# Window attention: row scores in one piece over four PSUM banks, and TensorE's loop run to the last group

## The chip, the cores and the metric

The kernel runs on one core of one Trainium2 chip. The metric is the time of one execution on the device, in microseconds (us); three executions give a median of 966.29 us (965.54 to 969.62). Engines are named as the profile names them: PE is the matrix engine (TensorE), PEld its weight loads, DVE is VectorE, ACT is ScalarE, POOL is GpSimd, SP is SyncE.

## The reference

The input x is 4 images of 128 channels, 112 x 112 pixels, float32. Each image is normalised in 32 groups of 4 channels. Then it is shifted by 3 pixels down and across, cut into 7 x 7 windows (49 tokens, 256 windows an image), and each window goes through attention with 8 heads of 16 channels; the result is shifted back and added to x.

```
def _L0_conv_ref(x, w_qkv, b_qkv):
    xs = jnp.roll(x, (-SHIFT, -SHIFT), axis=(-2, -1))
    qkv = jnp.einsum('bchw,oc->bohw', xs, w_qkv) + b_qkv[None, :, None, None]
    ...
    scores = jnp.einsum('bxyhqd,bxyhkd->bxyhqk', q, k) * scale
    attn = jax.nn.softmax(scores, axis=-1)
    out = jnp.einsum('bxyhqk,bxyhkd->bxyhqd', attn, v)
    ...
    return jnp.roll(out, (SHIFT, SHIFT), axis=(-2, -1))
...
x = x + _L0_conv_ref(_gn(x), L0_conv_w_qkv, L0_conv_b_qkv)
```

## The kernel before

The unit of work is a group: half of a band of windows, 8 windows of 49 tokens, 392 tokens in all. There are 128 groups (4 images, 16 bands, 2 halves), numbered g. The channels lie on the 128 partitions, as 4 pairs of heads of 32 partitions each. Precision is kept by splitting a float32 value into a high and a low float16 (or bfloat16) half, and three products stand for one.

Every engine has its own program: a function `step(g, ...)` that does its share for several groups at different stages, so that groups overlap like in a pipeline. The first and last steps are written out (with plain Python numbers, where `live` leaves out groups that do not exist), those between stand in a hardware loop (`Fori`) of two steps. Engines meet only through semaphores; each engine takes its instructions strictly in the order written, so a waiting instruction holds up all that stand behind it. The stages of a group:

- ACT `normalise` (L347) scales the pixels into xn, POOL `split_x` (L270) splits it in halves.
- PE `project_q`, `project_k`, `project_v` (L701, L695, L708) make q, k and v in PSUM. q and k share one bank (QK_BANK, 4) one after the other; ACT `evac_q`, `evac_k`, `evac_v` bring them out, DVE `low_q` (L557) takes q's low half, DVE `mask_q` (L562) lays q out twice, with the odd and with the even head of each pair put to zero, and POOL `split_k` (L279) splits k.
- PE `row_scores` (L722): scores with queries on the partitions, which serve for the maximum over the keys alone. A matmul takes the 32 rows of one pair of heads (a row tile of the array), 49 columns. One pair of heads fills one PSUM bank with its 8 windows. It is done in two pieces j = 0 and 1, two pairs of heads each, in the same banks 0 and 1. DVE `maximum` (L571) reduces each piece; piece 1 cannot start before the maximum of piece 0 is read.
- POOL `split_max` (L288), in two instructions (L293 and L296), PE `turn_max` (L738) and ACT `evac_neg` (L366) bring the negated maxima into a layout by columns.
- PE `column_scores` (L743): the scores again, transposed (keys on the partitions), on 32 x 64 tiles of the array, and on top of them (L760) the negated maxima. COL_BANKS are 6 and 7 for the first two pairs of heads and 2 and 3 for the others. ACT `exp` (L371) makes the probabilities, one call for each pair of banks.
- PE `sum_keys` (L765) sums over the keys, DVE `invert` (L577) takes the reciprocal, ACT `high_inverse` and DVE `low_inverse` split it, PE `spread_inverse` (L790) spreads it to all channels.
- PE `weigh` (L777) multiplies the probabilities with v into banks 6 and 7; ACT `evac_even` (L387), DVE `join` (L587) and DVE `scale_rows` (L595) put it together, POOL `add_image` (L299) adds x, and SP stores the band.

The order of PE's step (L801 to L822) is v(g), sums(g-2), turn(g-1), weigh(g-2), q(g+1), row scores 0 of g, inverse(g-2), column scores(g-1), row scores 1 of g, k(g+1). So three groups are in work on PE, and the maxima of g are used in the step after.

DVE also collects the statistics of the next image (`take_stats`, one chunk a step), and in four steps before an image ends it works out its normalisation in small dependent operations (`change_image`, L639), the first of them `gather_channels` (L511). SP loads the band of the image after next into a slot when the band there is stored.

## Time and profile before

| | |
|---|---|
| Median of three executions | 966.29 us |
| The profiled execution's own time | 967.17 us |
| Its span, first to last instruction | 965.3 us |
| PE busy | 897.0 us, 93% |
| PEld busy | 724.3 us, 75% |
| DVE busy | 738.2 us, 76% |
| ACT busy | 656.9 us, 68% |
| POOL busy | 597.7 us, 62% |
| DMA queue of SP | 51.59 MB, 15.1% of the 16 engines' span |
| Mean granted clock of PE | 0.986 of full speed |

Busy time is the union of an engine's instructions; matmuls are pipelined, so a busy PE tells only that there was always one under way. In the page's chain of waits, which goes back from the last instruction to what released each, 86% of the span is PE's. The first 36 us go to loading and to the statistics of the first image, in which PE has little to do.

### The profile page before, as it was taken

The page shows a single profiled execution, that of the slowest core. Times are in us where ns is not written, and L with a number is a line of the kernel's source. Part 1 is how long each engine was busy: PE and PEld are TensorE (multiplying, and loading weights), DVE is VectorE, ACT ScalarE, POOL GpSimd, SP SyncE. Part 2 cuts the span into 40 slices and gives each one's busy share as a digit, 9 for nine tenths or more (in the row PEclk, how much of TensorE's full clock was granted, in tenths as well). Part 3 has the DMA queues.
Part 4 walks back from the last instruction along what each step waited for, and adds up shares of the span by engine and source line. Part 5 has one row for each costly group of instructions (what it writes and reads, how often), then busy time and mean ns, then how long its engine had stood idle before and what let it go on. Part 6 is the DMA issues. An engine that isn't in the chain of part 4 may idle for free.

```text
span 965.3 us, 104413 instructions
## 1 busy us (share of the span) xinstructions
PE 897.0 (93%) x46595; PEld 724.3 (75%) x46595; DVE 738.2 (76%) x1404; ACT 656.9 (68%) x1297; POOL 597.7 (62%) x1067
## 2 busy tenths in 40 slices
PE   0479999999999999999999999999999999999984
PEld 0258888887788888888778888888778888888863
DVE  6667787877878787878878787878877777777762
ACT  1346777776677777777677777777677777777752
POOL 1335666666566767676576767676666767676741
PEclk9999999999999999999999999999999999999996
DMA  9401112112112211221121000000000000000011
GB/s 372 170 4 51 50 67 67 51 49 67 51 49 67 67 53 47 67 67 54 46 67 50 17 33 33 33 17 33 34 17 33 33 33 17 33 33 33 17 36 37
DMA packets 29920, 51.96 MB, mean 54 GB/s; under 512 B 3650, under 2 KB 28868, under 8 KB 29764
## 3 DMA queue, kind: packets, MB, share of 16 engines
q1 hardware_dynamic: 29892, 51.59, 15.1%
q8 instruction: 17, 0.28, 0.1%
q14 instruction: 11, 0.09, 0.0%
HBM read 25.89 MB, written 25.69 MB: 53 GB/s over the span
## 4 chain that ended last, share of the span: by engine, by line
PE 86%; DVE 8%; issue 4%; POOL 1%; ACT 1%; DMA 0%; POOLq 0%; SPq 0%; DVEq 0%; ACTq 0%
PE psum L733 16%; PE psum L785 12%; PE psum L753 11%; PE psum L771 10%; PE psum L717 8%; PE psum L705 8%; PE psum L698 7%; PE psum L797 4%; PE psum L760 3%; PE psum L713 3%; PE psum L740 2%; DVE neg_max L574 2%; DVE stats L494 2%; DVE q_halves L559 1%; DVE mixed L599 1%
## 5 line engine op out<-in xcount | busy, mean ns | idle before, releaser
L374 ACT ACTIVATE probs_t<-psum,exp_scale 128x800 f32<-128x800 f32 x256 | 223.6, 925 | 177.8 <-PE psum L760 177.8
L574 DVE TENSOR_REDUCE neg_max<-psum 100x16 f32<-100x784 f32 x256 | 249.5, 974 | 43.1 <-PE psum L733 18.3
L293 POOL TENSOR_SCALAR neg_halves<-neg_max 100x32 bf16<-100x32 f32 x128 | 60.5, 473 | 289.9 <-DVE neg_max L574 289.9
L733 PEld LDWEIGHTS psum<-k_hi,q_masks 32*128 32x128 f16 x8192 | 174.7, 91 | 47.6 <-issue 46.4
L733 PE MATMUL psum<-k_hi,q_masks 32*128 32x49 f16 x8192 | 197.4, 179 | 4.5 <-issue 2.7
L733 PE MATMUL psum<-k_lo,q_masks 32*128 32x49 f16 x4096 | 182.2, 179 | 0.0
L733 PEld LDWEIGHTS psum<-k_lo,q_masks 32*128 32x128 f16 x4096 | 160.5, 91 | 0.0
L306 POOL TENSOR_TENSOR stage<-mixed,image 128x343 f32 (+7 forms) x256 | 144.7, 586 | 10.7 <-DVE mixed L599 7.2
L351 ACT ACTIVATE xn<-image,shift_c,rstd_c 128x21 f32 (+6 forms) x256 | 132.5, 575 | 8.0 <-DVE shift_c L554 6.1
L753 PE MATMUL psum<-q_masks,k_hi 32*64 32x100 f16 x8192 | 129.1, 219 | 6.1 <-issue 3.5
L785 PE MATMUL psum<-probs_t,v_rows 64*32 64x100 f32 x8192 | 132.1, 254 | 1.7 <-issue 1.7
L579 DVE RECIPROCAL inv<-psum 128x49 f32<-128x49 f32 x128 | 60.0, 469 | 92.8 <-PE psum L771 92.8
L286 POOL TENSOR_TENSOR k_lo<-k,k_hi 128x392 f16<-128x392 f32 x128 | 116.5, 910 | 10.7
L276 POOL TENSOR_TENSOR xn_lo<-xn,xn_hi 128x392 f16<-128x392 f32 x128 | 116.3, 909 | 10.7
L771 PE MATMUL psum<-probs_t,sum_rows 128*32 128x49 f32 x8192 | 119.1, 210 | 3.0 <-ACT probs_t L374 3.0
L771 PEld LDWEIGHTS psum<-probs_t,sum_rows 128*32 128x32 f32 x8192 | 101.5, 112 | 16.6 <-ACT probs_t L374 3.3
L753 PE MATMUL psum<-q_masks,k_lo 32*64 32x100 f16 x4096 | 111.5, 218 | 1.7 <-issue 1.7
L753 PEld LDWEIGHTS psum<-q_masks,k_hi 32*64 32x64 f16 x8192 | 103.4, 102 | 11.8 <-issue 6.8
L785 PEld LDWEIGHTS psum<-probs_t,v_rows 64*32 64x32 f32 x8192 | 103.2, 106 | 9.1 <-issue 1.9
L591 DVE SCALAR_TENSOR_TENSOR summed<-psum,v_scale,even_out 128x392 f32<-128x392 f32 x128 | 78.8, 616 | 26.5 <-ACT even_out L391 26.5
L567 DVE TENSOR_SCALAR q_masks<-q_halves,even_odd 128x800 f16<-128x800 f16 x256 | 98.3, 427 | 0.2
L717 PE MATMUL psum<-w_lo,xn_hi 128*128 128x128 f16 x512 | 94.7, 222 | 0.7 <-issue 0.7
(120 smaller groups left out, 1867.8 us busy)
## 6 DMA issues: line engine op xcount, KB each, us to landing
out_dram<-stage SPq DMA_DIRECT2D x64, 224.0 KB, 2.1
out_dram<-stage SPq DMA_DIRECT2D x64, 168.0 KB, 1.9
image<-in_x_dram SPq DMA_DIRECT2D x32, 224.0 KB, 2.6
image<-in_x_dram SPq DMA_DIRECT2D x1, 6104.0 KB, 27.6
image<-in_x_dram SPq DMA_DIRECT2D x34, 168.0 KB, 2.5
image<-in_x_dram SPq DMA_DIRECT2D x6, 896.0 KB, 9.8
image<-in_x_dram SPq DMA_DIRECT2D x1, 728.0 KB, 14.5
w_nat<-in_L_conv_w_qkv_dram SPq DMA_DIRECT2D x1, 192.0 KB, 2.5
```

The source lines that it names most:

```text
L276: nc.gpsimd.tensor_tensor(xn_lo[:, par, :, 0:TOK], xn[:, :, :], xn_hi[:, par, :, 0:TOK], ALU.subtract).then_inc(x_split, 1)
L286: nc.gpsimd.tensor_tensor(k_lo[:, par, :, 0:TOK], k, k_hi[:, par, :, 0:TOK], ALU.subtract).then_inc(k_split, 1)
L306: last = nc.gpsimd.tensor_tensor(pixel_view(stage[:, bass.ds(st, BAND)], piece), token_view(mixed[:, half, :, :], piece), pixel_view(image ...
L351: last = nc.scalar.activation(token_view(xn, piece), pixel_view(image[:, bass.ds(at, BAND)], piece), ACT.Identity, bias=shift_c[:, 0:1], s ...
L374: nc.scalar.activation(probs_t[:, 2 * u:2 * u + 2, :, :].rearrange("p h a q -> p h (a q)"), psum[:, COL_BANKS[u], 0:PAIRS * ROWS2], ACT.Ex ...
L567: last = nc.vector.tensor_scalar(both[:, :, e, :], q_halves[:, :, :, :].rearrange("p l w q -> p (l w) q"), even_odd[:, e:e + 1], None, ALU ...
L574: nc.vector.tensor_reduce(neg_max[:, par, 2 * j:2 * j + 2, :], psum[0:ROWS2, ROW_BANKS, 0:GT] .rearrange("p h (w k) -> p h w k", k=TOK), A ...
L717: last = nc.tensor.matmul(psum[:, V_BANK, a * C:(a + 1) * C], xs[:, par, 2 * a:2 * a + 2, :].rearrange("p w k -> p (w k)"), wv[:, 2, :], s ...
L733: last = nc.tensor.matmul(psum[:, ROW_BANKS.start + h - 2 * j, w * TOK:(w + 1) * TOK], q_masks[rows, par, low + w * ROWS2:low + w * ROWS2 ...
L753: nc.tensor.matmul(psum[side, COL_BANKS[h // 2].start + h % 2, a * ROWS2:(a + 1) * ROWS2], k[rows, par, w, :], q_masks[rows, par, low + w ...
L771: last = nc.tensor.matmul(psum[c * PC:(c + 1) * PC, SUM_BANK, SPARE_SUM], sum_rows[:, a, e, :, :, :].rearrange("p t w s -> p (t w s)"), pr ...
L785: last = nc.tensor.matmul(psum[c * PC:(c + 1) * PC, OUT_BANKS.start + s, a * C:a * C + ROWS2], v_rows[side, par, a, c * PC:(c + 1) * PC], ...
```

## The change

- `row_scores` has no pieces: all four pairs of heads run in one sequence of 96 matmuls, each pair in a bank of its own, banks 0 to 3. One semaphore, row_mm, tells when it is done; both maxima wait for it, and read banks 0 and 1, and 2 and 3.
- The column banks swap: the first two pairs of heads now use banks 2 and 3, the others 6 and 7. The sums over keys move from bank 3 to the spare columns of bank 4, which q and k use.
- PE's step is rewritten: row scores(g), weigh(g-1), sums(g-1), v(g+1), turn(g), q(g+2), column scores(g), inverse(g-1), k(g+2). Waits follow: row scores(g) wait for the first exponential of g-1 and for maxima 0 and the negated maxima of g-1; column scores(g) wait for maximum 1 of g; sums(g-1) wait for k(g+1) to be evacuated; q(g+2) waits for the reciprocal of g-1.
- The steps of ACT and DVE are put in a new order, with q and k one group further ahead. POOL keeps its order.
- The scale and shift of the normalisation have two tiles, by turns for the images, since `normalise` runs one group further ahead.
- PE's loop runs to the last group, so that in steps 126 and 127 it also projects groups 128 and 129, which do not exist, from what lies in the tiles. Other engines raise the semaphores x_split, q_low, k_evac and v_evac by hand for them. One PE step stands behind the loop.
- The statistics of the next image start one band earlier, and `change_image` starts two steps earlier.

```diff
-        ROW_BANKS, COL_BANKS, OUT_BANKS = slice(0, 2), (slice(6, 8), slice(2, 4)), slice(6, 8)
-        NEG_BANK, SUM_BANK, QK_BANK, V_BANK, INV_BANK = 0, 3, 4, 5, 5
+        ROW_BANKS, COL_BANKS, OUT_BANKS = (slice(0, 2), slice(2, 4)), (slice(2, 4), slice(6, 8)), slice(6, 8)
+        NEG_BANK, QK_BANK, V_BANK, INV_BANK = 0, 4, 5, 5
...
             def exp(g, u):
                 act.wait_ge(col_mm, g + 1)
-                wait(act, out_mm, g)
+                wait(act, sum_mm, g)
...
@@ @block.scalar, step @@
+                if live(g + 1):
+                    evac_k(g + 1)
+                if live(g - 1):
+                    evac_even(g - 1)
+                if live(g + 3):
+                    normalise(g + 3, n + 1 + par, 1 - par, b)
+                if live(g - 1):
+                    high_inverse(g - 1)
+                if live(g + 1):
+                    evac_v(g + 1, 1 - par)
                 if live(g):
-                    evac_k(g)
+                    evac_neg(g)
                 if live(g + 2):
...
+                    evac_q(g + 2)
                 if live(g):
...
+                    exp(g, 0)
+                    exp(g, 1)
...
@@ @block.vector, step @@
+                if live(g + 1):
+                    mask_q(g + 1, 1 - par)
+                if live(g - 2):
+                    scale_rows(g - 2, par)
                 if live(g):
...
+                    maximum(g, par, 0)
+                    maximum(g, par, 1)
+                if live(g - 1):
+                    invert(g - 1)
+                    join(g - 1)
+                    low_inverse(g - 1)
                 for chunk in chunks:
                     take_stats(image_at + chunk * STAT, chunk)
...
+                if live(g + 2):
+                    low_q(g + 2)
...
+            def project_q(g, par):
+                pe.wait_ge(x_split, g + 1)
+                wait(pe, k_evac, g)
+                wait(pe, inv_done, g - 2)
...
-            def row_scores(g, par, j):
...
+            def row_scores(g, par):
+                pe.wait_ge(q_masked, g + 1)
+                pe.wait_ge(k_split, g + 1)
+                wait(pe, max_done[0], g)
+                wait(pe, neg_ready, g)
+                wait(pe, exp_done[0], g)
                 for w in range(GW):
                     for n, (low, k) in enumerate(((0, k_hi), (0, k_lo), (Q_LEN, k_hi))):
-                        for h in (2 * j, 2 * j + 1):
+                        for h in range(HP):
...
             def column_scores(g, par):
-                wait(pe, exp_done[1], g)
-                wait(pe, inv_done, g)
+                pe.wait_ge(max_done[1], g + 1)
                 wait(pe, join_done, g + 1)
...
             def sum_keys(g):
-                pe.wait_ge(exp_done[0], g + 1)
-                pe.wait_ge(exp_done[1], g + 1)
+                pe.wait_ge(k_evac, min(g + 3, GROUPS) if isinstance(g, int) else g + 3)
...
                 if live(g):
-                    project_v(g, par)
-                if live(g - 2):
-                    sum_keys(g - 2)
+                    row_scores(g, par)
                 if live(g - 1):
-                    turn_max(g - 1)
-                if live(g - 2):
-                    weigh(g - 2, par)
+                    weigh(g - 1, 1 - par)
+                    sum_keys(g - 1)
                 if live(g + 1):
-                    project_q(g + 1, 1 - par)
+                    project_v(g + 1, 1 - par)
                 if live(g):
-                    row_scores(g, par, 0)
-                if live(g - 2):
-                    spread_inverse(g - 2, live(g))
+                    turn_max(g)
+                if live(g + 2):
+                    project_q(g + 2, par)
+                if live(g):
+                    column_scores(g, par)
                 if live(g - 1):
-                    column_scores(g - 1, 1 - par)
-                if live(g):
-                    row_scores(g, par, 1)
-                if live(g + 1):
-                    project_k(g + 1, 1 - par)
-
-            for g in range(-1, 2):
+                    spread_inverse(g - 1, live(g + 1))
+                if live(g + 2):
+                    project_k(g + 2, par)
+
+            for g in range(-2, 2):
                 step(g, g & 1)
-            with pe.Fori(1, GROUPS // 2 - 1) as n:
+            with pe.Fori(1, GROUPS // 2) as n:
                 step(2 * n, 0)
                 step(2 * n + 1, 1)
-            for g in range(GROUPS - 2, GROUPS + 2):
-                step(g, g & 1)
+            step(GROUPS, 0)
```

## Rows read from the trace of the kernel before

**Rows 1.** Timeline of PE, one step: start us, us, engine, line, operation, tiles, shapes, count.
```profile
602.13 0.20 PE L733 MATMUL psum<-k_hi,q_masks 32*128 32x49 f16 x2
...
602.84 0.37 PE L797 MATMUL psum<-inv_rows,pick_head 128*128 128x49 f16 x8
...
603.14 0.25 PE L753 MATMUL psum<-q_masks,k_hi 32*64 32x100 f16 x8
...
604.08 0.35 PE L760 MATMUL psum<-neg_rows,pick_window 32*128 32x100 bf16 x16
...
604.27 0.18 PE L733 MATMUL psum<-k_hi,q_masks 32*128 32x49 f16 x2
...
604.96 0.34 PE L698 MATMUL psum<-xn_hi,w_hi 128*128 128x392 f16 x1
...
605.49 0.38 PE L713 MATMUL psum<-bias_rows,ones_rows 128*128 128x512 f16 x1
...
606.46 0.91 PE L771 MATMUL psum<-probs_t,sum_rows 128*32 128x49 f32 x64
...
607.30 0.22 PE L740 MATMUL psum<-ident,neg_halves 100*128 100x100 bf16 x1
...
607.45 1.02 PE L785 MATMUL psum<-probs_t,v_rows 64*32 64x100 f32 x64
...
608.40 0.34 PE L705 MATMUL psum<-xn_hi,w_hi 128*128 128x392 f16 x1
...
609.02 0.20 PE L733 MATMUL psum<-k_hi,q_masks 32*128 32x49 f16 x2
```

**Rows 2.** Timeline of all engines, same step: exponentials, last row scores, maximum, masks, split.
```profile
604.48 1.75 ACT L374 ACTIVATE probs_t<-psum,exp_scale 128x800 f32<-128x800 f32 x2 [1.30 <-PE psum L760]
...
604.85 0.18 PE L733 MATMUL psum<-k_hi,q_masks 32*128 32x49 f16 x2
...
605.07 0.97 DVE L574 TENSOR_REDUCE neg_max<-psum 100x16 f32<-100x784 f32 x1
...
605.96 0.76 DVE L567 TENSOR_SCALAR q_masks<-q_halves,even_odd 128x800 f16<-128x800 f16 x2
...
606.39 0.41 POOL L293 TENSOR_SCALAR neg_halves<-neg_max 100x32 bf16<-100x32 f32 x1 [2.22 <-DVE neg_max L574]
```

**Rows 3.** Timeline of PE, same step: column scores, eight matmuls in a row.
```profile
603.59 0.28 PE L753 MATMUL psum<-q_masks,k_lo 32*64 32x100 f16 x8
...
603.79 0.28 PE L753 MATMUL psum<-q_masks,k_lo 32*64 32x100 f16 x8
```

**Rows 4.** Timeline of PE near the start: turn, and q right behind it.
```profile
47.12 0.21 PE L740 MATMUL psum<-ident,neg_halves 100*128 100x100 bf16 x1
...
47.17 0.33 PE L705 MATMUL psum<-xn_hi,w_hi 128*128 128x392 f16 x1
```

**Rows 5.** Timeline, the step before rows 6: channels gathered, maximum, split.
```profile
233.47 0.90 DVE L514 BATCH_NORM_AGGREGATE agg<-stats 128x2 f32<-128x168 f32 x1
...
235.22 0.97 DVE L574 TENSOR_REDUCE neg_max<-psum 100x16 f32<-100x784 f32 x1
...
236.38 0.56 POOL L293 TENSOR_SCALAR neg_halves<-neg_max 100x32 bf16<-100x32 f32 x1 [3.29 <-DVE neg_max L574]
```

**Rows 6.** Timeline of all engines before the second image: maximum, split, turn.
```profile
242.85 0.97 DVE L574 TENSOR_REDUCE neg_max<-psum 100x16 f32<-100x784 f32 x1
...
244.16 0.22 POOL L293 TENSOR_SCALAR neg_halves<-neg_max 100x32 bf16<-100x32 f32 x1 [2.97 <-DVE neg_max L574]
...
244.46 0.25 POOL L296 TENSOR_TENSOR neg_halves<-neg_max,neg_halves 100x32 bf16<-100x32 f32 x1
...
244.76 0.22 PE L740 MATMUL psum<-ident,neg_halves 100*128 100x100 bf16 x1 [0.49 <-POOL neg_halves L296]
```

**Rows 7.** Timeline: the first row scores, and the last exponentials.
```profile
41.29 0.22 PE L733 MATMUL psum<-k_hi,q_masks 32*128 32x49 f16 x2
...
953.05 1.75 ACT L374 ACTIVATE probs_t<-psum,exp_scale 128x800 f32<-128x800 f32 x2 [2.54 <-PE psum L760]
```

More of the change, by code:

```diff
@@ L346, in _, with normalise @@
                                      scale=slot_of[:, w:w + 1]).then_inc(picks_made, 1)
-            def normalise(g, t, half):
+            def normalise(g, t, half, b):
                 wait(act, x_split, g)
@@ L351, in normalise @@
                     last = nc.scalar.activation(token_view(xn, piece), pixel_view(image[:, bass.ds(at, BAND)], piece),
[L352 removed]
+                                                ACT.Identity, bias=shift_c[:, b % 2:b % 2 + 1], scale=rstd_c[:, b % 2, 0:1])
                 last.then_inc(xn_ready, 1)
@@ L422, in _ @@
                 with act.Fori(b * BANDS - 1, (b + 1) * BANDS - 1) as n:
-                    step(2 * n, n, 0)
-                    step(2 * n + 1, n, 1)
-            for g in range(GROUPS - 2, GROUPS + 2):
+                    step(2 * n - 1, n - 1, 1, b)
+                    step(2 * n, n, 0, b)
+            for g in range(GROUPS - 3, GROUPS + 1):
                 step(g, g // 2, g & 1)
+                if g == GROUPS - 2:
+                    act.wait_ge(k_evac, GROUPS)
+                    act.sem_inc(k_evac, 1)
+                    act.wait_ge(v_evac, GROUPS)
+                    act.sem_inc(v_evac, 1)
         @block.vector
@@ L578, in invert @@
                 dve.wait_ge(sum_mm, g + 1)
-                nc.vector.reciprocal(inv32[:, :], psum[:, SUM_BANK, SPARE_SUM]).then_inc(inv_done, 1)
+                nc.vector.reciprocal(inv32[:, :], psum[:, QK_BANK, SPARE_SUM]).then_inc(inv_done, 1)
             def low_inverse(g):
@@ L654, in _ @@
             work_out_scales()
+            step(-2, -1, 0)
             step(-1, -1, 1)
@@ L658, in _ @@
             dve.wait_ge(loaded[1], 32)
-            step(2, 1, 0, (0, 1, 2), BANDS * BAND)
-            step(3, 1, 1, (3, 4, 5), BANDS * BAND)
-            with dve.Fori(2, BANDS - 3) as n:
-                two_steps(n, 2 * n + 2, BANDS * BAND)
+            step(2, 1, 0, (0, 1, 2, 3), BANDS * BAND)
+            step(3, 1, 1, (4, 5, 6, 7), BANDS * BAND)
+            with dve.Fori(2, BANDS - 4) as n:
+                two_steps(n, 2 * n + 4, BANDS * BAND)
             for b in (1, 2):
@@ L665, in _ @@
                 at = ((b + 1) % 2) * BANDS * BAND
-                first = b * BANDS - 1
-                for n in range(4):
+                first = b * BANDS - 2
+                for n in range(5):
                     dve.wait_ge(loaded[b + 1], 32 * -(-(2 * n + 2) * STAT // BAND))
@@ L693, in _ @@
             products = ((w_hi, xn_hi), (w_hi, xn_lo), (w_lo, xn_hi))
+            def project_q(g, par):
+                pe.wait_ge(x_split, g + 1)
+                wait(pe, k_evac, g)
+                wait(pe, inv_done, g - 2)
+                for n, (w, xs) in enumerate(products):
+                    last = nc.tensor.matmul(psum[:, QK_BANK, 0:GT], w[:, 0, :], xs[:, par, :, 0:TOK], start=n == 0, stop=n == 2)
+                last.then_inc(q_mm, 1)
             def project_k(g, par):
@@ L699, in project_k @@
                 last.then_inc(k_mm, 1)
-            def project_q(g, par):
-                pe.wait_ge(x_split, g + 1)
-                wait(pe, k_evac, g)
-                for n, (w, xs) in enumerate(products):
-                    last = nc.tensor.matmul(psum[:, QK_BANK, 0:GT], w[:, 0, :], xs[:, par, :, 0:TOK], start=n == 0, stop=n == 2)
-                last.then_inc(q_mm, 1)
             def project_v(g, par):
@@ L770, in sum_keys @@
                         for c in range(HP):
-                            last = nc.tensor.matmul(psum[c * PC:(c + 1) * PC, SUM_BANK, SPARE_SUM],
+                            last = nc.tensor.matmul(psum[c * PC:(c + 1) * PC, QK_BANK, SPARE_SUM],
                                                     sum_rows[:, a, e, :, :, :].rearrange("p t w s -> p (t w s)"),
@@ L778, in weigh @@
                 pe.wait_ge(v_evac, g + 1)
-                wait(pe, join_done, g + 1)
+                pe.wait_ge(exp_done[0], g + 1)
+                pe.wait_ge(exp_done[1], g + 1)
                 pe.sem_inc(waited_pe, 1)
```

76 lines of the change are left out of this document (23 added, 53 removed).

## The prediction

> **What bounds the kernel now.** I read one step of the loop as the matrix engine (PE) ran it, then the views of the other engines around the same step. In [rows 1] each of PE's pieces starts where the one before ends: row scores 602.13, inverse 602.84, column scores 603.14, maxima added 604.08, row scores 604.27, k 604.96, v 605.49, sums 606.46, turn 607.30, weigh 607.45, q 608.40, and the next row scores at 609.02. The step lasts 6.88 us and PE does not wait in it. PE is the bound; the other engines have gaps. Two loops run beside it that will matter. In [rows 2] the second maximum starts 0.22 us after the last matmul of row scores (604.85, 605.07), its successor 0.89 later (605.96), GpSimd's first half of the split at 606.39; the turn at 607.30 is 2.23 us after that maximum. The exponential starts at 604.48, 0.40 us after the first matmul that adds the maxima (604.08).
>
> **Part 1: row scores in one piece.** Removed: two pieces, 0.71 us (602.13 to 602.84) and 0.69 us (604.27 to 604.96), 1.40 together. Each is 48 matmuls in 24 rounds of two row tiles; 24 rounds take 604.27 to 604.85, 25 ns a round. Added: one piece of 96 in 24 rounds of four tiles. If a round still takes 25 ns it is 0.60 us, plus 0.11 to change over. No row shows four tiles with 49 columns. The nearest is column scores, also 96 matmuls with their weight loads, on eight tiles at once. They take 0.94 us up to the next piece, and their later matmuls come 24 in 0.20 us, 8.3 ns each ([rows 3]: eight from 603.59, sixteen between, then 603.79). A round of 100 columns on four tiles takes under 48 ns (four of them from 604.08 to 604.27), eight tiles at 8.3 ns take 67, so this looks like the pace at which instructions arrive and not like the array's. At this pace 96 take 0.80; I take 0.78, with 0.60 and 1.20 (no gain from four tiles) as ends. PE's sum goes from 6.88 to 6.88 - 1.40 + 0.89 = 6.37 us.
>
> The Trainium skill, "TensorE: Matmul & The Clock Gate", section "The mechanism", has row tiles start some 4 ns apart and overlap. By that a round of four stays at 25 ns and the piece at 0.60. [Rows 3] disagree for a long stream, and I weigh it as a rival.
>
> **Part 2: the order becomes a ring.** The order of PE in a step is now row scores(g), weigh(g-1), sums(g-1), v(g+1), turn(g), q(g+2), column scores(g), inverse(g-1), k(g+2). Row scores take banks 0 to 3, and banks 2 and 3 are also those of the first half of the column scores. So row scores(g+1) wait for the first exponential of g, which waits for column scores(g), and these come behind turn(g), which waits for both maxima of g. Before, one group's maxima had most of a step before they were needed; now one whole round of dependences must fit in one step. Its length, from the start of one group's row scores to that of the next:
> row scores 0.78; to the first maximum 0.22 [rows 2]; to the second 0.89, the spacing behind a maximum in [rows 2]; from there to the turn 1.84 (below); turn to q 0.05 as in [rows 4] (0.15 if turn keeps the changeover it has in front of weigh, 607.30 to 607.45); q to column scores 0.62 (608.40 to 609.02); column scores to the maxima 0.94; to the exponential 0.40; the exponential 0.93 (604.48 starts a pair of 1.75 us) and 0.05 to PE. Sum 6.72 us.
>
> **Maximum to turn, 1.84.** The 2.23 of [rows 2] hold something that the change moves away. There the first half of the split takes 0.41 us (0.56 for a group of the other parity, 236.38 in [rows 5]) while the masks of q (605.96, 0.76 us) run on VectorE, and it ends as they end. In [rows 6] two small operations of an image change stand between maximum and masks, the split gets in ahead of the masks and takes 0.22; its second half starts 0.30 after it (244.46), and the turn, for which PE was waiting, 0.05 after that half's end (244.76). From the maximum's end to the split it is 0.34 here (243.82 to 244.16) and 0.19 in the other parity (236.19 to 236.38, [rows 5]), 0.26 in the mean. In the changed order the masks run ahead of the maxima, and behind them the reciprocal, which reads PSUM. So 0.98 + 0.26 + 0.30 + 0.25 + 0.05 = 1.84. If the split stays long it is 2.11; with the steady rows' hand-over too, 2.23.
>
> The Trainium skill, "SBUF — State Buffer", section "Who interferes with whom", says that a VectorE operation with two operands in SBUF, too, holds off a reading GpSimd, and the other way round. This speaks against the change: the low half of the inverse now falls beside the split of k and may be held by it. In this kernel that would use up some of the 0.35 us that k has below; the sum stays.
>
> **What hides the rest.** In a step counted from its row scores: PE reaches the turn at 0.89 + 0.95 + 0.84 + 0.97 = 3.65 us, and the ring has it ready at 3.73: covered. k(g+2) waits for q evacuated and its low half taken: q ends 4.50, evacuated 5.1 (some 0.6 us for such an operation), low half 5.8, k 5.8 to 6.35, before the row scores at 6.72. Moving k behind the inverse so costs nothing; it has 0.35 us, and past this what is late next is VectorE's low half of q. The sums now wait for k's evacuation (1.25, needed at 1.85) because they share its bank, q for the reciprocal (3.3, needed at 3.8), column scores for the join (3.8, needed at 4.4). ScalarE: k, even outputs, normalise (up to 1.3 us), inverse, v, maxima, q follow to 5.1; the exponential's inputs are there at 5.75. GpSimd's order is kept; it splits k by about 5.1 for row scores at 6.72. Behind a waiting row-scores instruction on PE stand weigh and the sums, for which nobody is short. The doubled scale and shift tiles cost nothing. SP's stores and loads keep their order, and come once in two steps.
>
> **Start, image changes, end.** Before: first row scores 41.29 ([rows 7]) + 127 steps of 6.88 + 11.0 from a group's row scores to the end of its exponentials (602.13 to 604.48 + 1.75 one step later) + 10.5 from there (954.80, [rows 7]) to the end of the span 965.3 = 936.6. The other 28.7 us are stalls at the start, in three image changes, and in the last steps outside PE's loop. After: the first row scores stand behind k(1), whose wait for q's low half makes them 2.5 later, 43.8 (estimate). A group's exponentials end 7.5 after its row scores. Channel gathering (1.75 us between 233.47 and 235.22, [rows 5]) stands now at the end of VectorE's step, where about 0.9 us are free, so that an image change costs some 1.2 instead of 3. PE's loop runs to the last group and only one step stands outside it. Projections for groups 128 and 129 are in slots that the ring already counts or waits out; nobody waits for them. Of the 28.7 I keep 12 (ends 5 and 28.7). Sum: 43.8 + 127 x 6.72 (853.4) + 7.5 + 10.5 + 12 = 927.2 us of span; the execution lies 1.9 over its span (967.17), so 929. That execution is 0.9 over the median of 966.29, less than my steps can tell; I say 929.
>
> **The rivals.**
> A, the forecast, 929: 0.56.
> B, four tiles at 25 ns a round: ring 6.54, 127 x 0.18 = 23 less, 906. For it: the round of two is exactly that. Against: the pace in [rows 3]. 0.10.
> C, the split stays long because another VectorE operation holds it: ring 6.99, 34 more, 963. For it: 0.41 in the steady row; against: [rows 6]. 0.13.
> D, the slower side: the ring runs at the hand-overs of the steady rows, 2.23 from maximum to turn and 0.23 from exponential to PE (606.23 to 606.46; PE was never the waiting one there, so these may be just slack), and 0.15 after the turn. Ring 7.39, 85 more: 1014. It decides from a ring of 7.03 us, where 127 steps cancel what start and end save. Same sign: the four tiles do not overlap (1.20): 7.14, 982. Together 0.17.
> E, PE waits each step and its clock falls to the lower level at times; the rows of the start have such waits. Above 990. 0.04.
>
> **How the numbers follow.** What a measurement of this kernel can tell from no change is about 0.5%, here 4.8 us. A and B are faster (0.66), C lies at the bound, half of it faster, half within (0.07, 0.06). A's own range is 907 to 961 (steps 0.12 shorter or longer, 15 us, and the 12 between its ends), just to the bound. D and E slower, 0.21. Range: A, B and C hold 0.79: 903 to 965.
>
> **What would show it.** Right: steps of about 6.7 us in which PE waits before row scores for probs_t, some 0.3 us, and hardly before the turn; row scores some 0.8 us; the first half of the split near 0.22 us. Wrong: row scores at 0.6 or 1.2 (B, D); a split of 0.4 us (C); PE waiting before k or column scores; a lower granted clock in mid-span (E).

## The result: no faster, and the profile after

The changed kernel takes 970.65 us (median of 8 executions, 969.36 to 971.73) against 968.60 us (965.54 to 969.62, 8 executions) for the kernel before: a ratio of 1.0033, 95% interval 1.0020 to 1.0047. The forecast was 929 us with a range of 903 to 965; neither held. The profiled execution took 971.08 us with a span of 969.3 us, where my sum had 927.2: 42.1 us are missing.

The head of the page of the kernel after: busy time, and the granted clock of PE in 40 slices.

```profile
PE 859.5 (89%) x46620; PEld 649.5 (67%) x46620; DVE 752.5 (78%) x1404; ACT 671.2 (69%) x1297; POOL 586.5 (61%) x1067
...
PEclk9999999999999999999999999999999999999998
```

PE is 37.5 us less busy than before and the span is 4.0 us longer. So PE's work did shrink, and it turned into waiting. The granted clock stayed at 0.995 of full speed in the mean, so rival E is out. The view of waits of PE after says where it waits: engine, line, releaser, then us in total, times, longest.

```profile
PE psum L741 <- ACT probs_t L376: 37.4, 122, 0.3
...
PE psum L748 <- POOL neg_halves L296: 13.2, 13, 1.3
```

PE waits 122 times, some 0.3 us each, in front of the row scores (L741) for the exponentials. That is the wait that was forecast, and the order of PE is a ring as forecast. Only the ring is 6.95 us long, not 6.72. Two views of one of its rounds follow. First PE, as in [rows 1]:

```profile
600.79 0.24 PE L741 MATMUL psum<-k_hi,q_masks 32*128 32x49 f16 x8
...
600.89 0.25 PE L741 MATMUL psum<-k_hi,q_masks 32*128 32x49 f16 x8
...
601.21 1.01 PE L792 MATMUL psum<-probs_t,v_rows 64*32 64x100 f32 x64
...
604.08 0.22 PE L748 MATMUL psum<-ident,neg_halves 100*128 100x100 bf16 x1
...
604.27 0.33 PE L708 MATMUL psum<-xn_hi,w_hi 128*128 128x392 f16 x1
...
604.88 0.25 PE L760 MATMUL psum<-q_masks,k_hi 32*64 32x100 f16 x8
...
605.81 0.35 PE L767 MATMUL psum<-neg_rows,pick_window 32*128 32x100 bf16 x16
...
606.66 0.33 PE L714 MATMUL psum<-xn_hi,w_lo 128*128 128x392 f16 x1
...
607.29 0.21 PE L741 MATMUL psum<-k_hi,q_masks 32*128 32x49 f16 x4 [0.31 <-ACT probs_t L376]
...
607.35 0.23 PE L741 MATMUL psum<-k_hi,q_masks 32*128 32x49 f16 x8
...
607.42 0.23 PE L741 MATMUL psum<-k_hi,q_masks 32*128 32x49 f16 x8
```

Then the other engines in the same round, which answer to [rows 2] (the two maxima are one row here):

```profile
601.29 1.85 DVE L581 TENSOR_REDUCE neg_max<-psum 100x16 f32<-100x784 f32 x2 [0.52 <-PE psum L741]
...
603.48 0.22 POOL L293 TENSOR_SCALAR neg_halves<-neg_max 100x32 bf16<-100x32 f32 x1 [2.40 <-DVE neg_max L581]
...
603.78 0.24 POOL L296 TENSOR_TENSOR neg_halves<-neg_max,neg_halves 100x32 bf16<-100x32 f32 x1
...
606.22 1.75 ACT L376 ACTIVATE probs_t<-psum,exp_scale 128x800 f32<-128x800 f32 x2 [0.65 <-PE psum L767]
```

What the reader is to see: the split's first half takes 0.22 us and not 0.41, and the turn (604.08) starts 0.06 after the end of its second half (604.02). From the turn to q (604.27) it is 0.19 us, where [rows 4] have 0.05. And the first of the two exponentials that start at 606.22 ends at 607.15, where it releases PE, yet the row scores begin at 607.29.

Read over 26 steps in mid-span (mean, in us, each from the start of one piece to the start of the next), the ring stands against the terms of the forecast like this:

```
                               forecast   after
row scores to first maximum      1.00      1.02
first to second maximum          0.89      0.89
second maximum to turn           1.84      1.83
turn to q                        0.05      0.20
q to column scores               0.62      0.60
column scores to exponential     1.34      1.34
exponential to row scores        0.98      1.07
one step                         6.72      6.95
```

**The 42.1 us.** Steps: 127 x 0.23 = 29. The leftover of stalls: from the first row scores (43.92) to the last (951.79) it is 907.9, and 127 x 6.95 = 882.7, which leaves 25.2 where I kept 12: 13 more. Start and end are within 0.5 us. The leftover is 12.4 in the first four steps (counted from turn to turn, 40.17 us for four, against 27.8 of plain ones) and 12.4 in three image changes: the four steps that begin with the turns at 227.33, 235.09, 243.14 and 251.39 last 7.76, 8.06, 8.25 and 7.88 us, 4.1 over four plain ones, and so it goes three times. I had forecast 1.2 for each.

### The profile page after: what moved, and what is told of

Its sections match the earlier page's. It is cut to its first block and busy times, and to the rows that moved or that the text cites. A ratio compares the mean times of both kernels' runs of the same rounds, so it can differ in the third digit from the quotient of the medians.

```text
span 969.3 us, 104662 instructions
## 1 busy us (share of the span) xinstructions
PE 859.5 (89%) x46620; PEld 649.5 (67%) x46620; DVE 752.5 (78%) x1404; ACT 671.2 (69%) x1297; POOL 586.5 (61%) x1067
## 5 line engine op out<-in xcount | busy, mean ns | idle before, releaser
L581 DVE TENSOR_REDUCE neg_max<-psum 100x16 f32<-100x784 f32 x256 | 237.3, 968 | 75.6 <-PE psum L741 75.6
L293 POOL TENSOR_SCALAR neg_halves<-neg_max 100x32 bf16<-100x32 f32 x128 | 27.7, 216 | 307.0 <-DVE neg_max L581 307.0
L741 PEld LDWEIGHTS psum<-k_hi,q_masks 32*128 32x128 f16 x8192 | 110.5, 91 | 86.4 <-issue 47.7
L393 ACT ACTIVATE even_out<-psum,v_scale 128x392 f32<-128x392 f32 x128 | 75.2, 588 | 114.1 <-PE psum L792 114.1
L741 PE MATMUL psum<-k_hi,q_masks 32*128 32x49 f16 x8192 | 120.4, 185 | 37.8 <-ACT probs_t L376 37.4
L566 DVE SCALAR_TENSOR_TENSOR q_halves<-psum,q_bias,q_halves 128x392 f16<-128x392 f32 x128 | 80.4, 628 | 92.7 <-ACT q_halves L365 92.7
L574 DVE TENSOR_SCALAR q_masks<-q_halves,even_odd 128x800 f16<-128x800 f16 x256 | 115.9, 494 | 9.7 <-PE psum L767 2.4
L276 POOL TENSOR_TENSOR xn_lo<-xn,xn_hi 128x392 f16<-128x392 f32 x128 | 116.6, 911 | 10.7
L286 POOL TENSOR_TENSOR k_lo<-k,k_hi 128x392 f16<-128x392 f32 x128 | 116.4, 909 | 10.6
L741 PE MATMUL psum<-k_lo,q_masks 32*128 32x49 f16 x4096 | 112.8, 184 | 0.7 <-issue 0.7
L741 PEld LDWEIGHTS psum<-k_lo,q_masks 32*128 32x128 f16 x4096 | 99.5, 91 | 0.8 <-issue 0.8
L726 PE MATMUL psum<-w_hi,xn_hi 128*128 128x128 f16 x516 | 94.2, 220 | 1.0 <-issue 1.0
```

Of the source, the lines that this page charges most:

```text
L276: nc.gpsimd.tensor_tensor(xn_lo[:, par, :, 0:TOK], xn[:, :, :], xn_hi[:, par, :, 0:TOK], ALU.subtract).then_inc(x_split, 1)
L286: nc.gpsimd.tensor_tensor(k_lo[:, par, :, 0:TOK], k, k_hi[:, par, :, 0:TOK], ALU.subtract).then_inc(k_split, 1)
L574: last = nc.vector.tensor_scalar(both[:, :, e, :], q_halves[:, :, :, :].rearrange("p l w q -> p (l w) q"), even_odd[:, e:e + 1], None, ALU ...
L581: nc.vector.tensor_reduce(neg_max[:, par, 2 * j:2 * j + 2, :], psum[0:ROWS2, ROW_BANKS[j], 0:GT] .rearrange("p h (w k) -> p h w k", k=TOK) ...
L726: last = nc.tensor.matmul(psum[:, V_BANK, a * C:(a + 1) * C], xs[:, par, 2 * a:2 * a + 2, :].rearrange("p w k -> p (w k)"), wv[:, 2, :], s ...
L741: last = nc.tensor.matmul(psum[:, ROW_BANKS[h // 2].start + h % 2, w * TOK:(w + 1) * TOK], q_masks[rows, par, low + w * ROWS2:low + w * RO ...
```

## The experiments

All start from the changed kernel, which was not run again beside them; the kernel before was, with medians of 967.25 to 967.72 us (968.60 beside the changed kernel). Ratios are to the kernel before, measured beside each run, and a difference of 1.5 us to the changed kernel says nothing. "Step" is the mean over 26 plain steps in mid-span. The theory after the result, called W in the expectations: while PE's sequencer stands at an instruction that waits, the wait instructions queued behind it are dealt with only after the release, one by one, and each delays what follows. Where PE never waited, in the kernel before, they had been dealt with by then. The hardware's own records of the sequencer (start, duration in ns, instruction) in the round above, and at the place of [rows 4], speak for it:

```
kernel after, turn and q:
604075  95  weight load of turn (waits for the split)
604168  51  wait instruction: reciprocal done, k evacuated
604244  95  weight load of q
kernel after, row scores (exponential ends at 607148):
607186  51  wait instruction: exponential done, k split
607263  90  weight load of row scores (waits for the masks of q)
kernel before, at rows 4 (PE does not wait there):
46885   51  wait instruction: k evacuated
47066   98  weight load of turn
47122   99  weight load of q
```

In the first two blocks the wait instruction stands between the release and the work, takes 0.05 us itself, and the weight load behind it starts 0.08 us after its start. In the third it had been dealt with 0.18 us before the weight load of the turn, and only 0.06 us lie between the two weight loads.

**e2, q's waits ahead of the turn.** The two waits of q stand with the turn's own wait, in front of its weight load, where PE has time.

```diff
-            def project_q(g, par):
-                pe.wait_ge(x_split, g + 1)
+            def wait_q(g):
                 wait(pe, k_evac, g)
                 wait(pe, inv_done, g - 2)
+
+            def project_q(g, par):
+                pe.wait_ge(x_split, g + 1)
+                if isinstance(g, int) and g < 2:
+                    wait_q(g)
...
-            def turn_max(g):
+            def turn_max(g, q_next=False):
                 pe.wait_ge(neg_split, g + 1)
+                if q_next:
+                    wait_q(g + 2)
...
-                    turn_max(g)
+                    turn_max(g, live(g + 2))
```

> The same work as the changed kernel; q's waits for k's evacuation and for the reciprocal are dealt with in front of the turn, where PE arrives early and waits anyway, and q keeps one wait. Theory W: turn to q 0.05 to 0.10 instead of 0.197 us, step 6.95 -> 6.80 to 6.85, 13 to 19 us less, about 953 to 958. Rival C (0.197 is what the array needs to change over from the turn's 100-row matmul, as 0.148 in front of weigh in the kernel before): no change, 970.

Measured: 958.12 us (957.65 to 959.27), ratio to the kernel before 0.9901 (0.9885 to 0.9918). Step 6.848, 0.103 shorter. The span fell by 11.8, which is 115 x 0.103: the twelve steps of the three image changes gain nothing (see e3 and e4). In its timeline q now follows the turn by 0.08:

```profile
603.65 0.22 PE L754 MATMUL psum<-ident,neg_halves 100*128 100x100 bf16 x1
603.73 0.34 PE L712 MATMUL psum<-xn_hi,w_hi 128*128 128x392 f16 x1
```

No work was taken away; only two waits changed places. So 0.11 of the 0.15 us that turn to q was too long are the queued waits.

**e5, the exponential's wait alone on its instruction.** A semaphore increment between the other waits and this one makes the wait for the exponential ride on the first weight load itself.

```diff
             def row_scores(g, par):
...
                 wait(pe, neg_ready, g)
+                pe.sem_inc(waited_pe, 1)
                 wait(pe, exp_done[0], g)
```

> The same work as the changed kernel; in front of the row scores an extra semaphore increment takes the four waits that are long fulfilled, and the wait for the exponential stands alone behind it, so that the weight load carries it. (Written first it cost more: the register operation for the other waits' values took it, and two wait instructions came behind the release: exponential to row scores 0.21 instead of 0.145 us.) Theory W: 0.145 -> 0.06, step 6.95 -> 6.87, 11 us less, about 960. Rival (0.145 is what ScalarE's release to PE needs, whatever stands between): 970.

Measured: 960.81 us (960.77 to 961.70), ratio 0.9929 (0.9912 to 0.9946). Step 6.863, and the row scores start 0.98 us after the start of the exponential instead of 1.07 (0.98 is the forecast's term). PE's waits in front of them shrink from 0.31 to 0.22 us:

```profile
606.68 1.75 ACT L376 ACTIVATE probs_t<-psum,exp_scale 128x800 f32<-128x800 f32 x2 [0.65 <-PE psum L768]
...
607.67 0.20 PE L742 MATMUL psum<-k_hi,q_masks 32*128 32x49 f16 x4 [0.22 <-ACT probs_t L376]
```

**e1, the exponential's wait first.** The same idea, tried first and in a worse way: the wait moved to the head of `row_scores`.

```diff
             def row_scores(g, par):
+                wait(pe, exp_done[0], g)
                 pe.wait_ge(q_masked, g + 1)
...
-                wait(pe, exp_done[0], g)
```

> The same work as the changed kernel; of the five waits in front of the row scores the one for the first exponential is now written first, so that the weight load itself carries it and the other four are dealt with while PE waits. Theory W (the step is the ring of dependences, and waits that have to be dealt with after the release are part of it): from the exponential's end to the first row-scores matmul 0.06 instead of 0.145 us, step 6.95 -> 6.87, 127 x 0.085 = 11 us less, about 960. Rival R (the step is set by something else, PE's own work or VectorE, and the wait for the exponential only fills a gap): no change, 970.

Measured: 978.50 us (977.84 to 980.13), ratio 1.0118 (1.0101 to 1.0135), slower, where I expected faster. Step 7.016. From the exponential's start to the row scores it is 1.14 in the mean, but the two parities differ. In every second step the weight load itself carries the wait, as meant, and starts the row scores 0.06 us after the exponential's end (0.15 in the kernel after). In the others the compiled program has the wait on an instruction that computes a register for the other waits, and two wait instructions behind it are dealt with after the release: 0.35 to 0.39 us. The sequencer's records of such a step:

```
kernel e1, row scores (exponential ends at 610914):
610952  36  register operation, which waits for the exponential
611048  51  wait instruction: maximum 0 read
611154  51  wait instruction: negated maxima evacuated, k split
611231  90  weight load of row scores
```

The expectation missed, and W holds in both parities: less behind the release, 0.09 us less; more behind it, 0.20 us more.

**e9, both waits (e2 and e5).**

> The changed kernel with both edits to the waits (q's waits dealt with ahead of the turn, the exponential's wait alone in front of the row scores). Each alone took 12.5 and 9.8 us. Theory W (all of it lies on one ring, so the savings add): step 6.95 -> 6.76, 22 to 24 us less than 970.65, about 948, 2% below the kernel before. Rival (with a shorter ring something else sets the step, PE's own 6.4 us and its waits for k or the join first): 955 or more.

Measured: 948.18 us (947.54 to 949.38), ratio 0.9794 (0.9774 to 0.9815). Step 6.762, the sum of the two gains (0.10 and 0.09). The span fell by 21.7, again 115 steps' worth. With the waits away the ring is 0.04 over my 6.72: 0.02 from row scores to the first maximum and 0.02 from turn to q. This is the change as it was meant, and it is worth 2.1% (interval 1.85 to 2.26).

**e3, the masks behind the maxima.** In the forecast, 0.27 us of the way from maximum to turn went with the masks of q, which had stood beside the split (rival C). Here they come back, between the maxima and the reciprocal.

```diff
-                if live(g + 1):
-                    mask_q(g + 1, 1 - par)
...
                     maximum(g, par, 0)
                     maximum(g, par, 1)
+                if live(g + 1):
+                    mask_q(g + 1, 1 - par)
```

> The same work; VectorE makes the masks of q right behind the two maxima, as the kernel before did behind its second maximum, and not ahead of them. If the masks hold the split of the maxima on GpSimd (the prediction's step on 1.84 us): the split's first half 0.4 to 0.56 instead of 0.216 us, maximum to turn 2.1 instead of 1.83, ring 0.27 longer, and the reciprocal 0.67 later, which holds q back by up to 0.3 more: 34 to 70 us more, 1005 to 1040. Rival (the short split of the changed kernel has another cause): split stays 0.22, and only the reciprocal's delay shows, up to 35 us more.

Measured: 997.45 us (996.95 to 997.95), ratio 1.0309 (1.0289 to 1.0330). Step 7.220, 0.27 longer, all of it between second maximum and turn (2.10 instead of 1.83). The split starts beside the masks and ends 0.08 us after them (605.73 and 605.65), as in [rows 2]:

```profile
604.89 0.76 DVE L574 TENSOR_SCALAR q_masks<-q_halves,even_odd 128x800 f16<-128x800 f16 x2
605.32 0.41 POOL L293 TENSOR_SCALAR neg_halves<-neg_max 100x32 bf16<-100x32 f32 x1 [2.56 <-DVE neg_max L581]
```

The step that read this from [rows 6] was right, and worth 0.27 us a step. 127 x 0.27 = 34.3, but the span grew by only 26.9. Part of the rest is that the four steps of an image change are no plain ones: they take 31.9 to 32.0 us together in the kernel after and in e1, e2, e5, e6, e7 and e9 alike, whether a plain step is 6.76 or 7.27, so what changes the ring counts in the 115 others. And here, with the maxima ahead of the masks, the four take 30.3, which no run took apart.

The Trainium skill, "SBUF — State Buffer", section "Who interferes with whom", says that a `tensor_scalar` of VectorE can run in a mode with both ports, and that of it and a GpSimd instruction the one issued first then has the shared ports for its whole length and blocks the other. The trace agrees: GpSimd's operation takes 0.41 us when it starts in the masks (604.89 to 605.65; 0.56 in the other parity) and 0.22 in the kernel after.

**e6, row scores in pairs of tiles.** One piece over four banks, but each bank pair finished before the next begins: what four tiles at once are worth.

```diff
-                for w in range(GW):
-                    for n, (low, k) in enumerate(((0, k_hi), (0, k_lo), (Q_LEN, k_hi))):
-                        for h in range(HP):
+                for w, n, (low, k), h in [(w, n, lk, h) for j in range(2) for w in range(GW)
+                        for n, lk in enumerate(((0, k_hi), (0, k_lo), (Q_LEN, k_hi))) for h in (2 * j, 2 * j + 1)]:
```

> The same work; the 96 row-scores matmuls run as before the change, two pairs of heads first and then the other two, still in four banks and under one semaphore. If the piece of four tiles is on the ring (the prediction's first term): its first to last start 1.2 instead of 0.78 us, step 6.95 -> 7.37, 53 us more, about 1024. Rival (PE is not what the step waits for): up to 10 more.

Measured: 1008.15 us, ratio 1.0415 (1.0394 to 1.0436). Step 7.273, 0.32 longer where 0.42 was expected, all of it between row scores and first maximum. PE's timeline, first and last of the piece:

```profile
600.25 0.20 PE L740 MATMUL psum<-k_hi,q_masks 32*128 32x49 f16 x2 [0.31 <-ACT probs_t L376]
...
601.36 0.18 PE L740 MATMUL psum<-k_hi,q_masks 32*128 32x49 f16 x2
```

From first to last start it is 1.12 us in the mean, against 0.75 in the kernel after. So four tiles do run faster than two, but by a third and not by half. In the timeline of the kernel after, twelve matmuls (the eight shown and four with k_lo) go by in 0.075 us at the beginning of the piece (607.35 to 607.42), 6.2 ns each: that is rival B's 25 ns a round. Later it is 0.10 (600.79 to 600.89), 8.3 ns each, the pace of the column scores in [rows 3]. Over 40 steps the first 24 starts are 6.5 ns apart in the mean and the rest 8.0 to 8.8. B was right for the first quarter of the stream and wrong for the rest.

**e4, no image change.** It leaves out the normalisation of images 1 to 3 (image 0's scale and shift serve for all), and so shows what the image changes cost.

```diff
-                step(2 * n, n, 0, after=lambda: gather_channels(b))
-                step(2 * n + 1, n, 1, after=group_variance)
-                step(2 * n + 2, n + 1, 0, first=guess_root, after=lambda: refine_root(1))
-                step(2 * n + 3, n + 1, 1, first=lambda: refine_root(NEWTON - 2), after=lambda: offer(b))
+                step(2 * n, n, 0)
+                step(2 * n + 1, n, 1)
+                step(2 * n + 2, n + 1, 0)
+                step(2 * n + 3, n + 1, 1, after=lambda: offer_again(b))
```

> Leaves out the working out of the normalisation of images 1 to 3 (all images are scaled with the figures of the first), statistics are still collected. Theory: the four steps before each image last 4.1 us longer than four plain ones because VectorE's small operations overrun its 0.7 us of slack in each: 3 x 4.1 = 12 less, about 958. Rival (the long steps come from the code there being written out and fetched for the first time): at most half of that goes, 965 or more.

Measured: 958.28 us, ratio 0.9905 (0.9885 to 0.9924), 12.4 us less than the kernel after: three times 4.1. The steps at the image changes are plain ones here (27.8 us for four). So in the other runs VectorE's work for the image change, and not the ring, sets these four steps: they stay at 31.9 to 32.0 us whatever the ring does, and the shorter the ring, the more an image change costs over plain steps.

**e8, the image change ahead of q's low half.** VectorE has its longest gap in front of `low_q`, so its small operations were put there (`before=` puts them there), and the refinements into one step.

```diff
-                step(2 * n, n, 0, after=lambda: gather_channels(b))
-                step(2 * n + 1, n, 1, after=group_variance)
-                step(2 * n + 2, n + 1, 0, first=guess_root, after=lambda: refine_root(1))
-                step(2 * n + 3, n + 1, 1, first=lambda: refine_root(NEWTON - 2), after=lambda: offer(b))
+                step(2 * n, n, 0, before=lambda: gather_channels(b))
+                step(2 * n + 1, n, 1, before=lambda: (group_variance(), guess_root()))
+                step(2 * n + 2, n + 1, 0, before=lambda: refine_root(NEWTON - 1))
+                step(2 * n + 3, n + 1, 1, before=lambda: offer(b))
```

> The same work; VectorE's small operations of an image change stand ahead of q's low half, where VectorE waits up to 1.1 us for ScalarE, and not behind it. The image change now costs 4.1 us over four plain steps. Theory (it overran 0.7 us of slack in each of four steps): the slack is 1.1 larger, 4.1 -> about 1, 9 us less, about 961. Rival (each small operation delays something else, whatever its place): no change, 970.

Measured: 976.77 us (975.25 to 978.54), ratio 1.0093 (1.0072 to 1.0114), slower, where I expected faster. The four steps are 7.45, 7.83, 9.02 and 9.29 at the first image change, 5.8 us over plain ones (5.8 and 6.6 at the other two). Timeline of VectorE, and under it that of GpSimd in the same stretch:

```profile
242.07 0.16 DVE L545 TENSOR_TENSOR rs_t<-rs 128x8 f32<-128x8 f32 x1
242.27 0.81 DVE L546 SCALAR_TENSOR_TENSOR rs_t<-rs_t,g_var 128x8 f32<-128x8 f32 x1
243.12 0.90 DVE L547 SCALAR_TENSOR_TENSOR rs<-rs_t,rs 128x8 f32<-128x8 f32 x1
...
244.53 0.17 DVE L546 SCALAR_TENSOR_TENSOR rs_t<-rs_t,g_var 128x8 f32<-128x8 f32 x1
```

```profile
242.16 0.91 POOL L286 TENSOR_TENSOR k_lo<-k,k_hi 128x392 f16<-128x392 f32 x1
243.02 0.98 POOL L306 TENSOR_TENSOR stage<-mixed,image 128x392 f32 x1
```

An operation on 8 numbers a partition takes 0.17 us when it starts between two operations of GpSimd (at 244.53, between 244.49 and 244.57) and 0.81 or 0.90 when it starts in a long one, and it ends within 0.02 us of that one (243.08 and 243.07, 244.02 and 244.00). The Trainium skill, "SBUF — State Buffer", section "Who interferes with whom", has this as a rule: a VectorE instruction with two inputs in SBUF contends with a GpSimd instruction that reads SBUF. The trace agrees. It holds for the kernel after, too, where one of these operations (L545) has 0.77 us (246.25 to 247.02) beside GpSimd's L276 that ends at 247.00. I had weighed this rule for the low half of the inverse alone. The gap that I filled was one in which GpSimd has its long operations.

**e7, the last two steps written out.** The loop ends one round earlier, and the last steps are separate code as in the kernel before.

```diff
-            with pe.Fori(1, GROUPS // 2) as n:
+            with pe.Fori(1, GROUPS // 2 - 1) as n:
...
-            step(GROUPS, 0)
+            for g in range(GROUPS - 2, GROUPS + 1):
+                step(g, g & 1)
```

> The changed kernel with TensorE's loop ending one turn earlier: steps 126 and 127 are written out, without work for groups that do not exist. If the longer steps at the end of the kernel before (3 to 4 us each over the others) came from code fetched for the first time, they are back: 5 to 8 us more, 976 to 979. Rival (they came from the order there, whose tail had few things left to overlap): within 2 us, 971.

Measured: 979.38 us (977.62 to 980.81), ratio 1.0123 (1.0106 to 1.0140). From turn to turn the last two steps are 9.92 and 10.14 us, against 6.88 in the kernel after: 6.3 us, and the span is 6.5 longer. PE's timeline there shows it stopped in mid-piece for nothing that another engine does ("issue"):

```profile
944.53 0.75 PE L792 MATMUL psum<-probs_t,v_rows 64*32 64x100 f32 x38
947.10 0.56 PE L792 MATMUL psum<-probs_t,v_rows 64*32 64x100 f32 x26 [1.81 <-issue]
```

The DMA view, from 900 to 970 us, tells of the queue that brings instructions, first for this run and then for the kernel after:

```profile
q8 instruction: 7, 0.11, 0.8%
q8 instruction: 1, 0.02, 0.1%
```

Only PE's code was changed. From 944 us on, 16 KB come every 3.6 to 4.1 us, while PE stands still at times. From 100 to 900 us, in the loop, this queue moves nothing in either run. So new code is what these steps wait for, as far as the trace can tell. The loop up to the last group is worth 6 to 9 us by itself, and the two groups that do not exist cost nothing that could be seen: the last three loop steps are as long as the others.

**e10, q ahead of the turn (with e5's increment).** If the waits of q are what follows the turn, q itself can go in front of it, so that the turn is followed by column scores at once and q fills time in which PE waited for the split.

```diff
-                if live(g):
-                    turn_max(g)
                 if live(g + 2):
                     project_q(g + 2, par)
                 if live(g):
+                    turn_max(g)
+                if live(g):
                     column_scores(g, par)
```

> The changed kernel with q projected ahead of the turn and not behind it, and the exponential's wait alone. q (0.60 us) leaves the stretch between turn and column scores, but PE reaches the turn 0.6 us later than it is ready, so PE's own work takes the ring's place there: row scores to turn 0.94 + 0.94 + 0.84 + 0.98 + 0.6 = 4.3 us against 3.73 for the maxima, then 0.15 to change over. Theory (the ring is then PE's work from row scores to the maxima added, 4.3 + 0.05 + 0.15 + 0.94, and 0.41 + 0.98): step about 6.8, 950. Rival (q was just idle filling on the ring, so all of its 0.6 us is won): 6.3, PE's own sum of 6.4 bounds it, 905.

Measured: 937.84 us (937.13 to 939.38), ratio 0.9687 (0.9664 to 0.9711): faster than both kernels, and faster than expected. PE's timeline:

```profile
605.46 0.33 PE L708 MATMUL psum<-xn_hi,w_lo 128*128 128x392 f16 x1
...
605.63 0.21 PE L749 MATMUL psum<-ident,neg_halves 100*128 100x100 bf16 x1
...
605.77 0.25 PE L761 MATMUL psum<-q_masks,k_hi 32*64 32x100 f16 x8
...
608.09 0.20 PE L742 MATMUL psum<-k_hi,q_masks 32*128 32x49 f16 x4
```

The split's second half had ended at 605.03 (it starts at 604.79 and lasts 0.24), so the turn at 605.63 waits for nothing. From row scores to column scores PE now goes through its own work without a wait, 4.34 us against 4.44 in e9. Step 6.670, 0.092 less than e9, 10.6 in 115 steps; the span is 10.0 less, with first steps 0.4 us longer and image changes 0.2 shorter each. What bounds it is PE's own order for the first two thirds of the step and, from column scores on, the chain to the exponential.

## Why the prediction was wrong, step by step

**The ring as the bound: right.** Step by step it is the forecast's, and five of its seven terms are within 0.02 us. Neither did another operation hold the split (C; it takes 0.22 us), nor did all of the stream go at 25 ns a round (B).

**"turn to q 0.05 as in [rows 4]": failed, it is 0.20.** 127 x 0.15 = 19 us. The row was read in a place where PE was late for the turn, so that q's wait was over before. In the ring PE is early. I had named 0.15 for this term as a case, but for another reason. The kernel after shows both cases itself. Near its start PE comes late to one turn, q's wait instruction is dealt with at 58.62, ahead of it, and q follows by 0.05; in the steady step PE waits, and q follows by 0.20:

```profile
58.88 0.21 PE L748 MATMUL psum<-ident,neg_halves 100*128 100x100 bf16 x1
58.93 0.33 PE L708 MATMUL psum<-xn_hi,w_hi 128*128 128x392 f16 x1
```

e2 took 0.11 of it back by moving two waits and nothing else.

**"the exponential 0.93 and 0.05 to PE": failed in its second half, it is 0.15.** 127 x 0.10 = 12 us. Same cause; e5 took 0.09 back. The slower rival D had these two terms (0.15 behind the turn, 0.23 before row scores) beside two that did not come. I wrote that the second "may be just slack" and gave the case 0.17; with these two alone the ring would have been 6.72 + 0.10 + 0.18 = 7.00, close to the 6.95 measured and to the 7.03 from which the change does not pay.

**"an image change costs some 1.2": failed, it is 4.1.** Three times 2.9 is 9 us. It even rose against the kernel before, where the four steps from 229.05 to 259.86 are 3.3 over plain ones. I counted the free time of VectorE in one step and placed only the gathering in it. But four steps carry such operations, each step has slack of its own and none of the step before, and some of the small operations are themselves slower beside GpSimd (0.17 us becomes 0.8). The four steps take 32 us whatever the ring; in a ring of 6.72 us they would have cost 5.1 (estimate, 32.0 - 4 x 6.72). VectorE's timeline of the kernel after shows the second of these steps: 2.2 us of operations in front of the masks.

```profile
236.62 0.63 DVE L566 SCALAR_TENSOR_TENSOR q_halves<-psum,q_bias,q_halves 128x392 f16<-128x392 f32 x1 [1.44 <-ACT q_halves L365]
237.16 0.28 DVE L530 SCALAR_TENSOR_TENSOR work_a<-g_sum,mean_row 128x32 f32<-128x32 f32 x1
...
238.56 0.76 DVE L540 TENSOR_SCALAR rs<-half_bits 128x8 int32<-128x8 int32 x1
...
239.36 0.77 DVE L574 TENSOR_SCALAR q_masks<-q_halves,even_odd 128x800 f16<-128x800 f16 x2
```

**The start: too small, 4 us.** I left the rest of the 12 for it; it is 12.4. The first four steps are written out, and PE's "issue" waits in them look like those of e7: seven between 53.8 and 78.0 us, 9.5 us together (1.97 at 57.77 is the longest), and the instruction queue brings ten pieces of 16 KB between 45 and 84 us. The kernel before has four such waits there, 5.7 us together, and eight pieces. No run took them apart, so the cause stays a likeness.

**The end: right.** From the last row scores to the end it is 17.5 us, where 18.0 were forecast, and the loop to the last group gave what was expected (e7).

The order of the sizes: the two hand-overs 31 us, image changes 9, start 4, together 44; the other terms of the ring and the tail take 2 back. With the hand-overs right alone, the forecast would have been 929 + 31 = 960, 11 below what was measured.

**The two parities: W once more, on GpSimd.** In the kernel after, second maximum to turn is 1.75 and 1.90 us in turn, and the steps are 6.87 and 7.03. The sequencer's records of GpSimd show why. With one parity nothing stands between the maximum's end and the split, and the split starts 0.19 us after it. With the other, two wait instructions and a register operation are dealt with after the release, and it is 0.34:

```
kernel after, GpSimd (second maximum ends at 603141):
603177  17  wait instruction: maximum 1 done
603243  32  register operation, which waits for maximum 0
603318  17  wait instruction: turn of the group before done
603479 216  split, first half
```

For the last four groups, which are written out in GpSimd's program, it is 0.19 with both parities, and the last steps are 6.87 and 6.88. The forecast had both values (0.34 and 0.19) and took their mean, so this costs it nothing; but some 0.08 us a step could be had there (an estimate, half of 0.15), and no run tried it. In e10, where the turn no longer stands in the ring, the difference is still there and does not show in the steps.

## What to carry to other kernels

When a change turns an engine that was never waiting into one that waits each step, look at what stands right behind each new blocking instruction: waits that used to be dealt with ahead are now paid after the release, some 0.1 us for each wait instruction, every step. Put the waits that are long satisfied in front of the one that blocks, and let the late one stand alone on the instruction it guards. Then look in the compiled program or the sequencer's records at where it landed: e1 had it right in every second step alone. Better still, put work of the same engine in front of it. A hand-over read from a profile is valid only for the case in which the engine is early or late as it will be.

## What the runs showed of the hardware that I had not expected

- A wait instruction of PE takes 0.05 us, and what follows it starts about 0.08 after its start. It is free when PE is behind and costs 0.09 to 0.11 us in the ring (e5, e2). With two of them and a register operation behind the release it was 0.35 us from the exponential's end to the row scores, instead of 0.15 with one and 0.06 with none (e1). On GpSimd, two and a register operation raise the hand-over from 0.19 to 0.34.
- Row tiles with 49 columns: 96 weight loads and matmuls take 0.75 us from first to last start on four tiles and 1.12 on two (e6). On four, the first quarter goes at 6.5 ns each, the rest at some 8.3.
- Steps written out behind the loop cost PE about 3 us each, with some 360 matmuls and their weight loads (e7: 9.92 and 10.14 against 6.88), while the instruction queue brings 16 KB every 3.6 to 4.1 us. That matters at the end of a kernel as much as at its start.
- A VectorE operation on 8 numbers a partition can take five times as long, 0.81 to 0.90 us instead of 0.17, when it starts in a long operation of GpSimd (e8).
